# Query and key stacks moved by pairs of heads, one semaphore for each pair, with slot tables to match

## What is computed

```python
x = x + _L0_xattn_ref(_layernorm(x), ctx_2048, ...)   # 128 latents, one attention, layernorm over all
x = x + _L0_ffn_ref(_layernorm(x), ...)               # 512x512 linear, 8 low-rank experts, top 2
x = x + _L1_xattn_ref(_layernorm(x), ctx_2048, ctx_2048, gamma)
x = x + _L1_ffn_ref(_layernorm(x), ...)               # 64 experts, top 8 of them for each of 4096 rows
```

```python
qh = q.reshape(B, 8, 32, 512); kh = k.reshape(B, 8, 32, 512); vh = v.reshape(B, 8, 32, 512)
sm = softmax(einsum('bhdq,bhdl->bhql', qh, kh) / sqrt(32))
ret = einsum('bhql,bhdl->bhdq', sm, vh)
```

## Time and profile before

| | us |
|---|---|
| median of 3 executions | 1871.05 (1867.81 to 1871.11) |
| profiled execution | 1886.31 |
| span of its profile | 1884.6 |
| PE busy | 1662.4 (88%) |
| DVE busy | 1204.7 (64%) |
| ACT busy | 1004.6 (53%) |
| POOL busy | 965.5 (51%) |
| mean granted clock of PE | 0.938 of full |

### The profile page before, as it was taken

The page is one execution under the profiler, slowest core; times in us unless marked ns, Lnnn a source line. Parts: engine busy times, 40 slices in busy tenths (PEclk is TensorE's granted clock), DMA queues, the critical chain, the costliest instruction groups (busy, mean ns, idle before and its releaser), DMA issues.

```text
span 1884.6 us, 25957 instructions
## 1 busy us (share of the span) xinstructions
PE 1662.4 (88%) x8576; PEld 1083.1 (57%) x8576; DVE 1204.7 (64%) x2706; ACT 1004.6 (53%) x1970; POOL 965.5 (51%) x882
## 2 busy tenths in 40 slices
PE   5778899999999999999999997826999999999984
PEld 2444454554554554544454543426998888888884
DVE  2465577677677676777677776334776666665662
ACT  3345556556556555656556654413655555555552
POOL 3121234463473473463473463665766666666665
PEclk9888999999999999999999998857999999999998
DMA  4578763443542532522422312026999999999995
GB/s 120 162 232 303 219 202 109 140 155 89 161 140 92 159 115 90 146 77 85 124 65 80 108 39 58 21 88 199 257 254 259 261 245 257 249 247 247 264 238 80
DMA packets 139732, 303.32 MB, mean 161 GB/s; under 512 B 27385, under 2 KB 29305, under 8 KB 139598
## 3 DMA queue, kind: packets, MB, share of 16 engines
q1 hardware_dynamic: 100686, 230.23, 39.8%
q0 software_dynamic: 38912, 71.43, 17.1%
HBM read 132.60 MB, written 155.91 MB: 153 GB/s over the span
## 4 chain that ended last, share of the span: by engine, by line
PE 55%; DMA 19%; issue 11%; DVE 7%; POOL 3%; SPq 3%; ACT 1%; another core or an unknown queue 0%; POOLq 0%; DVEq 0%; ACTq 0%
DMA out_rows<-y_slots,row_ids 14%; PE bank L670 7%; PE bank L683 6%; PE bank L661 6%; PE bank L642 3%; PE bank L582 3%; PE bank L603 3%; PE bank L705 2%; DMA x<-in_x 2%; PE bank L698 2%; PE bank L596 2%; PE bank L734 2%; PE bank L790 2%; PE bank L792 1%; PE bank L791 1%
## 5 line engine op out<-in xcount | busy, mean ns | idle before, releaser
L1190 DVE TENSOR_REDUCE max_col<-bank 128x1 f32<-128x512 f32 x512 | 346.9, 685 | 219.5 <-PE bank L661 209.4
L946 ACT ACTIVATE p_t<-bank 128x512 f32<-128x512 f32 x512 | 302.2, 599 | 250.9 <-PE bank L670 211.3
L1419 POOL TENSOR_TENSOR p_sum<-p_t 128x512 f32<-128x512 f32 x128 | 162.3, 1281 | 387.3 <-ACT p_t L946 386.7
L1478 POOL DMA_INDIRECT out_rows<-y_slots,row_ids x128 | 227.9, 1781 | 198.3 <-DMA out_rows<-y_slots,row_ids 157.7
L1431 POOL DMA_INDIRECT slot_rows<-row,slot_i x256 | 271.2, 1060 | 83.4 <-issue 76.5
L670 PE MATMUL bank<-q_stack,k_stack 98*128 98x512 f32 x512 | 283.1, 554 | 14.1 <-DMA q_stack<-max_lo 9.9
L661 PE MATMUL bank<-k_stack,q_stack 96*128 96x512 f32 x512 | 222.5, 436 | 47.6 <-issue 43.3
L1468 POOL TENSOR_TENSOR down_lo<-down,down_hi 96x1024 fp32r<-96x1024 f32 x64 | 188.4, 2944 | 16.1 <-DVE down_hi L1350 16.1
L790 PE MATMUL bank<-gate_up_hi,x_slots_t_hi 128*128 128x384 f32 x512 | 185.5, 362 | 0.5 <-DVE x_slots_t_lo L1319 0.5
L1319 DVE TENSOR_TENSOR x_slots_t_lo<-bank,x_slots_t_hi 128x512 fp32r<-128x512 f32 x128 | 88.3, 690 | 152.5 <-ACT x_slots_t_hi L1003 152.1
L670 PEld LDWEIGHTS bank<-q_stack,k_stack 98*128 98x128 f32 x512 | 102.2, 200 | 135.6 <-issue 122.5
(11 more groups left out here) (175 smaller groups left out, 3295.8 us busy)
## 6 DMA issues: line engine op xcount, KB each, us to landing
gate_up<-in_gate_up SPq DMA_DIRECT2D x64, 768.0 KB
slot_rows<-row SPq DMA_DIRECT2D x64, 577.0 KB, 7.3
x_slots<-slot_rows SPq DMA_DIRECT2D x64, 577.0 KB
k_stack<-prob SPq DMA_DIRECT2D x192, 128.0 KB
down<-in_down SPq DMA_DIRECT2D x64, 384.0 KB
q_stack<-x_t SPq DMA_DIRECT2D x128, 128.0 KB
x<-in_x SPq DMA_DIRECT2D x16, 512.0 KB
ctx<-in_ctx SPq DMA_DIRECT2D x16, 512.0 KB, 3.8
```

What stands on the lines that cost most here:

```text
L946: e.activation(p_t[step % 2][:, h, :], psum[n % 2][:, :], ACT.Exp, scale=SCALE).then_inc(free[n % 2], 1)
L1190: e.tensor_reduce(max_col[quad % 2][:, h, c:c + 1], psum[2 + n % 2][:, :], X, ALU.max, negate=True).then_inc(free[2 + n % 2], 1)
L1478: e.indirect_dma_start(out=out, out_offset=bass.IndirectOffsetOnAxis(ap=row_ids[e_ % NI][:, q, :].bitcast(U32), axis=0), in_=ye[e_ % NY][: ...
```

## The change

Three things. `stack_rows` takes one pair of heads (hq, hq + 4) with all its three parts, and each pair of q and of k has a semaphore of its own. A score waits for its own pair: scores 0 to 3 of a batch each wait for one. The readers that overwrite the sources wait for all four. And all tables have new numbers. SP's k and q events now wait for both the high and the low part.

```diff
-TENSOR = {"theta": -2.25, "phi": 10.25, "g": 10.5, "s0": 11, "t0": 20.75, "lat0": 23.75, "s1": 11, "t1": 21,
-          "lat1": 25.25, "s2": 11, "t2": 22.5, "lat2": 25.25, "s3": 11, "t3": 22.75, "lat3": 25.5, "mean": 27.5,
-          "v0": 28, "o0": 30.25, "v1": 42.25, "o1": 30.25, "x0": 35.25, "b00": 38.25, "b01": 38.75, "b02": 39,
-          "b03": 40, "f0": 41, "x1": 36.25, "b10": 39.25, "b11": 40.25, "b12": 40.5, "b13": 41.25, "f1": 41.25,
-          "lora": 38.25, "gated": 40.25}
...
+TENSOR = {"theta": 10.5, "phi": 10.5, "g": 12, "s0": 11, "t0": 18, "lat0": 20, "s1": 11, "t1": 19, "lat1": 23.25,
+          "s2": 11.25, "t2": 22.25, "lat2": 25, "s3": 13, "t3": 24, "lat3": 25.5, "mean": 27.5, "v0": 41.5, "o0": 31,
+          "v1": 42.75, "o1": 31, "x0": 35, "b00": 38.5, "b01": 40.25, "b02": 40.25, "b03": 40.75, "f0": 41,
+          "x1": 36.75, "b10": 40.25, "b11": 40.25, "b12": 40.25, "b13": 41, "f1": 41, "lora": 39.25, "gated": 40.5}
...
-GPSIMD = {"rstd": 7.5, "res0": 9.25, "res1": 22.75, "lat_rstd": 28, "rstd2": 33.75, "rstd4": 42}
-SYNC = {"ctx": -12.5, "x": 4.75, "k_hi0": 42, "k_hi1": 42.25, "k_lo": 42.5, "q_hi0": 42.75, "q_hi1": 43, "q_lo": 44}
...
+GPSIMD = {"rstd": 7.25, "res0": 9.5, "res1": 10.75, "lat_rstd": 28, "rstd2": 34.5, "rstd4": 42.25}
+SYNC = {"ctx": -11.75, "x": -5.5, "k0": 41.5, "k1": 42.5, "k2": 42.75, "k3": 42.75, "q0": 43, "q1": 43, "q2": 45.5,
+        "q3": 45.75}
...
-        k_in = [sem(f"k_in{i}") for i in range(2)]
-        q_in = [sem(f"q_in{i}") for i in range(2)]
+        k_in = [[sem(f"k_in{i}_{hq}") for hq in range(HPH)] for i in range(2)]
+        q_in = [[sem(f"q_in{i}_{hq}") for hq in range(HPH)] for i in range(2)]
...
-            def stack_rows(b, dst, part, n, done):
-                for hq in range(HPH):
+            def stack_rows(dst, parts, hq, done):
+
+                for n, part in enumerate(parts):
                     e.dma_start(dst[n * DQ:(n + 1) * DQ, hq:NHEAD:HPH, :].bitcast(F32),
-                                part[hq * DQ:(hq + 1) * DQ].bitcast(F32)).then_inc(done[b % 2], 16)
+                                part[hq * DQ:(hq + 1) * DQ].bitcast(F32)).then_inc(done[hq], 16)
...
-                elif what == "prep" and ev[2] in ("q_hi0", "q_hi1"):
+                    stack_rows(k_st[b % 2], (k_hi, k_hi, k_lo), int(ev[2][1]), k_in[b % 2])
+                elif what == "prep" and ev[2][0] == "q":
                     stacks_free(b)
                     w.wait_ge(q_hi_ok, 2 * b + 2)
-                    stack_rows(b, q_st[b % 2], q_hi, 2 * int(ev[2][4]), q_in)
-                elif what == "prep" and ev[2] == "q_lo":
-                    stacks_free(b)
                     w.wait_ge(q_lo_ok, 2 * b + 2)
-                    stack_rows(b, q_st[b % 2], q_lo, 1, q_in)
+                    stack_rows(q_st[b % 2], (q_hi, q_lo, q_hi), int(ev[2][1]), q_in[b % 2])
...
-                if n % BC == 0:
-                    w.wait_ge(q_in[b % 2], 16 * 3 * HPH * (b // 2 + 1))
-                    w.wait_ge(k_in[b % 2], 16 * 3 * HPH * (b // 2 + 1))
+                if n % BC < HPH:
+                    w.wait_ge(q_in[b % 2][h], 16 * 3 * (b // 2 + 1))
+                    w.wait_ge(k_in[b % 2][h], 16 * 3 * (b // 2 + 1))
...
+            def stacked(done, b):
+
+                for hq in range(HPH):
+                    w.wait_ge(done[b % 2][hq], 16 * 3 * (b // 2 + 1))
...
```

More of the change, by code:

```diff
@@ L46 @@
 PREPARE = 64
-TENSOR = {"theta": -2.25, "phi": 10.25, "g": 10.5, "s0": 11, "t0": 20.75, "lat0": 23.75, "s1": 11, "t1": 21,
[3 rows of a table removed]
-          "lora": 38.25, "gated": 40.25}
-SCALAR = {"xn0": 9, "xn1": 9, "xn20": 34, "xn21": 34.25, "xn40": 42.25, "xn41": 42.25, "theta": -0.75, "phi": 10.75,
[4 rows of a table removed]
-VECTOR = {"stats0": 6, "stats1": 6, "s0": 11.25, "r0": 11.75, "s1": 11.25, "r1": 14.25, "s2": 11.25, "r2": 14.75,
[3 rows of a table removed]
-GPSIMD = {"rstd": 7.5, "res0": 9.25, "res1": 22.75, "lat_rstd": 28, "rstd2": 33.75, "rstd4": 42}
-SYNC = {"ctx": -12.5, "x": 4.75, "k_hi0": 42, "k_hi1": 42.25, "k_lo": 42.5, "q_hi0": 42.75, "q_hi1": 43, "q_lo": 44}
[L64 to L68, removed]
+TENSOR = {"theta": 10.5, "phi": 10.5, "g": 12, "s0": 11, "t0": 18, "lat0": 20, "s1": 11, "t1": 19, "lat1": 23.25,
[3 rows of a table added]
+SCALAR = {"xn0": 8, "xn1": 9.25, "xn20": 34.75, "xn21": 34.75, "xn40": 42.5, "xn41": 42.5, "theta": 10.75,
[4 rows of a table added]
+VECTOR = {"stats0": 4.75, "stats1": 6, "s0": 11.25, "r0": 12.25, "s1": 11.25, "r1": 12.5, "s2": 11.5, "r2": 14,
[3 rows of a table added]
+GPSIMD = {"rstd": 7.25, "res0": 9.5, "res1": 10.75, "lat_rstd": 28, "rstd2": 34.5, "rstd4": 42.25}
+SYNC = {"ctx": -11.75, "x": -5.5, "k0": 41.5, "k1": 42.5, "k2": 42.75, "k3": 42.75, "q0": 43, "q1": 43, "q2": 45.5,
+        "q3": 45.75}
+TENSOR_OUT = {"x0": 41, "x1": 41, "route": 42, "place": 44}
+SCALAR_OUT = {"x0": 41.25, "x1": 41.75, "exp": 42.5}
+VECTOR_OUT = {"stats0": 4.75, "stats1": 22.75, "rows0": 25.75, "rows1": 25.75, "peak": 42.25, "top0": 42.75,
+              "top1": 42.75, "top2": 42.75, "place0": 45.75, "place1": 46, "place2": 46}
+GPSIMD_OUT = {"rstd": 25, "send": 65}
 SYNC_OUT = {"out": 22}
-TENSOR_TAIL = {"sums0": -1, "sums2": -1, "sums1": 2.5, "turn": 10.75, "inv": 16}
-SCALAR_TAIL = {"heads": 2.5, "sums": 5.75, "expand": 15.75}
-VECTOR_TAIL = {"turn": 11, "inv": 17.25, "add": 17.25}
+TENSOR_TAIL = {"sums0": -2.5, "sums2": -1.75, "sums1": 1, "turn": 11, "inv": 15.75}
+SCALAR_TAIL = {"heads": 4.5, "sums": 6.5, "expand": 12.75}
+VECTOR_TAIL = {"turn": 11.25, "inv": 16, "add": 17.5}
 TENSOR_MAX = {"max": 1.25}
@@ L77 @@
 VECTOR_MAX = {"max_lo": 1.75}
-SYNC_MAX = {"max": 7.5}
+SYNC_MAX = {"max": 5.75}
 WEIGHTED = 6.25
@@ L468, in _ @@
                         load_ctx(b)
-                elif what == "prep" and ev[2] in ("k_hi0", "k_hi1"):
+                elif what == "prep" and ev[2][0] == "k":
                     stacks_free(b)
                     w.wait_ge(k_hi_ok, 2 * b + 2)
-                    stack_rows(b, k_st[b % 2], k_hi, int(ev[2][4]), k_in)
-                elif what == "prep" and ev[2] == "k_lo":
-                    stacks_free(b)
                     w.wait_ge(k_lo_ok, 2 * b + 2)
-                    stack_rows(b, k_st[b % 2], k_lo, 2, k_in)
-                elif what == "prep" and ev[2] in ("q_hi0", "q_hi1"):
+                    stack_rows(k_st[b % 2], (k_hi, k_hi, k_lo), int(ev[2][1]), k_in[b % 2])
+                elif what == "prep" and ev[2][0] == "q":
                     stacks_free(b)
                     w.wait_ge(q_hi_ok, 2 * b + 2)
-                    stack_rows(b, q_st[b % 2], q_hi, 2 * int(ev[2][4]), q_in)
-                elif what == "prep" and ev[2] == "q_lo":
-                    stacks_free(b)
                     w.wait_ge(q_lo_ok, 2 * b + 2)
-                    stack_rows(b, q_st[b % 2], q_lo, 1, q_in)
+                    stack_rows(q_st[b % 2], (q_hi, q_lo, q_hi), int(ev[2][1]), q_in[b % 2])
                 elif what == "tail":
@@ L872, in prepare @@
                     if c == 0 and b:
-                        w.wait_ge(k_in[(b - 1) % 2], 16 * 3 * HPH * ((b - 1) // 2 + 1))
+                        stacked(k_in, b - 1)
                     w.wait_ge(neg_max_ok, C * b + c + 1)
@@ L899, in prepare @@
                     if b:
-                        w.wait_ge(q_in[(b - 1) % 2], 16 * 3 * HPH * ((b - 1) // 2 + 1))
+                        stacked(q_in, b - 1)
                     norm_apply(xn2, xb, row_rstd, row_off, int(what[3]), xn2_ok)
```

1 line of the change is left out of this document (removed), and 14 rows, old and new, of tables (SCALAR, VECTOR).

## The result

The changed kernel takes 1821.97 us (median of 4, 1821.15 to 1832.02) beside 1871.08 us for the kernel before on the same chip: ratio 0.9751, interval 0.9721 to 0.9782, 49 us less. The forecast was 1838 us. The profiled execution of the changed kernel took 1832.02 us (span 1830.3), against 1886.31 us before: 54.3 us less.

A forecast was written before the change was run, and what follows sets the result against it. TensorE and what makes it wait were taken to bound the middle. 3.75 - 1.0 - 0.6 = 2.15 us a batch, 26 over twelve, plus 8 at the edges: 34 us off 1886.31, scaled and said as 1838 us; range 1812 to 1868.

The forecast's parts named there:

- The wait ahead of score 0: TensorE's wait before each batch's first score in the middle goes: 2.35 us, with the clock 3.75 us a batch.
- the price of a pair's transfers: On SyncE's queue: three issues of 0.63 us, then 2.75 to land; pair 0 lands 11.7 us behind `f1`.
- rival 4: GpSimd late: slow sends delay `rstd4` by 2.7 us and what stands behind it; slower, 1886 us; chance 0.08.
- The cover: TensorE's other work between `f1` and the next batch's score 0: 13.6 us, a margin of 1.9 us over pair 0.
- own signs of being wrong: Pair 0 later than 13.6 us behind `f1`, a period at 67.3 us, or half clock without long waits.
- case 2: No new waits: the whole 3.75 us a batch go, 53 us with the edges, 1818 us; chance 0.2.
- The clock: TensorE's half clock behind the wait costs 1.4 us a batch and goes with the gap.
- The residual step: From `o0` to `x0`, new TensorE waits at `inv` (0.6 us) and score 22 (0.4): 1.0 us a batch, bounds 0 and 2.5.
- The small ones: New TensorE waits of 0.2 us at `gated` and 0.4 at `v0`: 0.6 us a batch, bounds 0 and 1.2.
- k, theta behind the norm: Early `k_lo` and k transfers lie beside TensorE; theta's copy behind `xn4` costs nothing, bounds 0 and 1.3 us.
- The edges: Outside the middle: 6 us for two early waits, 3 last batch, -2.5 start, 1.5 final sends; sum 8 us.
- Case 3: The wait moves: new waits of say 3.5 us a batch eat the gain, only edges remain; 1861 us, chance 0.13.

The follow-up runs named there:

- Send57: The changed kernel with the sends in slots 57.25 to 72.25 instead of from 65; 0.9734 of the kernel before, the changed kernel of the same set 0.9681.
- filler experiment: The kernel before with two idle fp32 matmuls added ahead of each batch's score 0; ratio 0.9907 to the kernel before, 18.6 us less.
- experiment 2: The kernel before with the pairs and their waits, k_lo early on VectorE and SyncE's slots as in the change; ratio 0.9724 to the kernel before.
- Experiment 1: The kernel before with the pairs and their waits, all tables old except SyncE's, which has the pairs; ratio 1.0238 to the kernel before.
- before_again: The kernel before, unchanged, run once more for a second trace; 0.9999 against itself, period 71.7 us.
- after_again: The changed kernel, unchanged, run once more for a second trace; ratio 0.9681 to the kernel before, period 67.4 us.
- experiment 6: The changed kernel with batch 14's routing 13 slots sooner, its sends 28 and batch 13's sends 16 sooner; ratio 0.9822, slower than the changed kernel.

## Why the prediction was right and wrong, point by point

**The wait ahead of score 0: right that it goes, wrong that all of it goes.** It went from 2.45 to 0.65 us a batch, and 0.29 came at score 1, where none was forecast. The step that failed is the price of a pair's transfers. Pair 0 was forecast to land 11.7 us behind the end of `f1` and landed at 14.5 in batch 6, from

```profile
471.05 1.02 PE L642 MATMUL bank<-lora_out,gated_t 65*128 65x512 f32 x2
```

to the landing at 486.55. 0.6 us of it are a later start of the q issues (7.7 us behind `f1` instead of 7.1): POOL's root starts behind one more send, the small form of rival 4. The other 2.2 us are the transfers. Pair 1 was forecast at 13.6 and landed at 18.5 in this batch, just behind the 18.2 at which PE was ready for score 1. The price was read from the last four issues of a queue, at a time when the kernel before had ended its sends; the first issues of the same queue, beside the sends, are the ones that pair 0 takes over, and the new table moved the sends four slots further onto them. Send57 shows the price without sends (2.3 us from issue to landing), the changed kernel the one with them (3.6). The cover was forecast at 13.6 and measured at 13.0. By the prediction's own signs of being wrong this counts: pair 0 came later than 13.6 us behind `f1` in batches 4 to 9 (13.8 to 14.5), and the period of 67.5 us is nearer to case 2's 67.3 than to the forecast's 68.9.

On the transfer itself the Trainium skill, "DMA: Bandwidth & Descriptors", section "Anatomy of one DMA", was nearer than the row that I used: the estimate from its fit, made for GpSimd's path, is 2.3 us for 128 KB, and the trace of send57 has 2.3 on SyncE's, where pair 0 lands 10.6 to 11.0 us behind `f1` in batches 4 to 14 (10.7 by the price of the Trainium skill). The same page of the Trainium skill, section "Queues, rings and completion order", says that each DMA engine goes round the queues it has work for, packet by packet, which would price two queues at once above one alone; the landings of 3.6 and 2.3 us agree with that, though no run here shows the engines' turns.

**The clock: right.** Forecast 1.4 us a batch, 1.33 us less busy time in the traces, 2.0 us in the filler experiment.

**The residual step: wrong, no new wait.** Forecast 1.0 us at `inv` and at score 22. PE in batch 6:

```profile
449.40 1.88 PE L610 MATMUL bank<-theta,out_w 128*128 128x512 f32 x4
451.27 0.66 PE L711 MATMUL bank<-ident,sum_sb 128*128 128x128 f32 x4
```

and DVE's part of `o0`, which frees the bank for `inv`:

```profile
450.46 0.75 DVE L1122 SCALAR_TENSOR_TENSOR x<-bank,out_b,x 128x512 f32<-128x512 f32 x1 [0.17 <-PE bank L610]
```

DVE is done 1.8 us behind the start of `o0` (forecast 1.9), but PE gets to `inv` (L711) only after 1.9 us and not after 1.4, so there is no gap. Score 22 shows none either. The row for L615 in the earlier trace rows has 1.98 us for both halves of `o0` and `o1`, so the 1.4 was short already there. The 1.0 us was the sum of two margins finer than the rows bear.

**The small ones: wrong in sign.** Forecast 0.6 us more a batch; 0.8 us less came. At `v0` there is 0.24 us where I had 0.4. At `gated` there is nothing, and the waits of the dispatch transposes and the router, 0.9 us a batch with that of `gated`, went. I had followed the steps that the change might hurt and never asked of the existing waits whether their own table entries had moved. They had, and experiment 2, which keeps those entries, keeps the waits.

Per batch: 2.15, less 0.95 for the waits at scores 0 and 1, plus 1.0, plus 0.36 for the small ones, plus 1.05 for the waits that went, is 3.61, and 3.62 were measured. (The wait of before was 0.10 more than the 2.35 of the sum, the clock gave 0.07 less than its 1.4; these cancel.)

**k, theta behind the norm:** free, as forecast. Experiment 1 shows what k costs if `k_lo` isn't moved, which my part on k had only as a step that "lies beside PE": it is the table edit on which the change depends.

**The edges: forecast 8 us in sum, measured 17.8 in the first pair of traces and 9.9 in the second; near it there, and by luck.** From the start to the first score of batch 3 the gain was 6.3 us in the first pair of traces, 12.3 in the second, before_again against after_again (forecast 3.5). From the first score of batch 15 to the start of the experts the first pair has 11.5 us (147.6 before, 136.1 after; forecast 4.5), but before_again takes 133.9 us there against 136.3 in after_again: without the 11.7 us of DVE and what goes with them nothing was gained at the end. Part of that is bookkeeping: with the changed tables more of a batch's work stands behind its first score (366 matmul records instead of 348 from there to the last weighted product), so it counts in another stretch. I had also taken POOL's 32 sends in a row as what ends the stretch; experiment 6 left this untested, since its own edit brought a longer wait. The last batch's wait ahead of score 0 went from 5.5 to 4.1 us, where I took 3 us off.

**The rivals.** Case 2 (no new waits, 1818) was nearer to the measured 1822 than the forecast (1838), and its reason was the better one: nearly all hand-overs of banks stayed hidden. What kept the kernel from it was the price of pairs 0 and 1, which was part of no case. That 1822 lies in the range all the same is in part luck: too little was expected to stay at the scores, too much to come elsewhere, and the two errors have opposite signs. With the sends at 61 the period is 66.4 us, below the 67.3 of case 2. Case 3 (the wait moves) is what experiment 1 shows; k_lo's new place prevented it.

## What to carry to other kernels

Take the duration of a transfer from a row with the same company: what else is on the DMA engines at that slot after the change, not in the place where the row stood. When an order is split finer, look at which of the old queue's places the first piece takes over, and at what frees its source: here the pairs paid only once the k rows left `prob` in time. Before pricing what an edit may break, list the waits that exist and look whether their entries move; and a queue entry put sooner can be reached long before its input is there, with everything behind it held.

## What the runs showed of the hardware that was not expected

A 128 KB transfer between SBUF rows took 2.3 us (median) from issue to landing with no sends beside it and 3.6 us (median; up to 5.5 for the third of pair 0, up to 7.1 for that of pair 1) beside indirect sends, one every 1.28 us. In batch 12 pair 0 landed in 2.8 us although POOL issued sends as densely: in the 3 us from 888 the queue of POOL's transfers moved

```profile
q0 software_dynamic: 80, 0.02, 2.9%
```

against, in the 3 us from 479 of batch 6,

```profile
q0 software_dynamic: 93, 0.35, 31.0%
```

(packets, MB, share of the 16 engines). This points to the sends' bytes as what slows the pairs, not their issue; that late rows find their expert full and are dropped would explain the few bytes, and no run here tests it. And 32 matmuls that compute nothing of use, two a batch, made a kernel 18.6 us faster, because they kept the clock up.
